# Values and scores of every fourth visit in one gap, and projected blocks copied out by ScalarE ahead of the rotary steps on VectorE

## The chip, the cores and the metric

The kernel runs on one core of one Trainium2 chip. The metric is the device time of one execution in microseconds (us); several executions are timed and their median is given. Engines are named as in the profile: PE (TensorE; PEld is its weight load), DVE (VectorE), ACT (ScalarE), POOL (GpSimd), SP (SyncE, which issues most transfers).

## The reference

A "macaron" transformer block on x of 4 x 1024 tokens with 256 features, in float32:

```
x = x + 0.5 * moe(layernorm(x))     # 32 experts, inner size 96, every expert computed for every token,
                                    # weighted by a thresholded top-8 softmax of x @ gate_weight.T
x = x + attention(layernorm(x))     # 16 query heads, 4 key/value heads, head size 16, rotary q and k,
                                    # softmax(q k^T / 4) v over 1024 keys, then Wo
x = x + 0.5 * moe(layernorm(x))
```

An expert computes `silu(x @ Wg.T) * (x @ Wu.T)`, its result goes through its down weights and is scaled by the token's weight for that expert. The rotary step replaces q by `q * cos + rotate_half(q) * sin`, and k likewise.

## The kernel before, in words

**Slots.** Both expert layers together are 384 slots (`SLOTS`), 24 for each group of 512 tokens (`PER_GROUP`); k is the group index d // 24 and s = d % 24 the slot within it. In slot d PE issues three blocks of 12 matmuls: the gate projection of step d+1 (line 1211, PSUM bank `B_G`), the up projection of step d+1 (line 1211, bank `B_U`) and the down projection of step d-1 (line 1229). ACT takes tanh of the gate result (line 668), DVE multiplies (`gated`, line 937, then `product`, line 945), POOL weighs by the expert's weight (line 601), ACT rounds to 16 bits (line 675), POOL forms the remainder (line 606), and the down projection uses both.

**Gaps and visits.** Attention runs in the gaps between these blocks: gap 0 after the gate block, gap 1 after the up block, gap 2 after the down block. One visit v is half a step of attention. PE issues two score matmuls for the row maxima of fill v + 40 (`score_max`, line 1241, 48 rows of the array) and, in other rows of the array at the same time, two score matmuls for the exponentials of v (`score_exp`, line 1253, 50 rows). DVE reduces each of the two banks of the first kind (`maximum`, line 960), ACT takes exponentials from each of the two banks of the second kind (line 691). A score matmul waits until the last contents of its bank have been taken, half by half (`max_taken`, `exp_done`). On every visit with v % 4 == 1 PE first issues two "quads" of the values (line 1274: four tiles of 32 array columns over all 128 rows, float32), and then the visit's scores. The table `VISIT` says which gap has which visit: three visits a slot while v < 0 (only maxima), then two a slot (gaps 0 and 1) and a third in gap 2 in every fifth slot. `SLOT_OF` is its inverse, and the slots for loads, output turns and output projections follow from it. The visits lie in slots 64 to 310.

**Events.** An event at the end of a slot uses bank `B_U` (`B_O` outside the attention), one ahead of the down block uses `B_G`. The event "join" projects normalised rows to one of three blocks of a group of 512 tokens (block 0: keys and values, blocks 1 and 2: queries; line 1193), in the slots s = 8, 10, 13 of k = 1 and 2 and s = 10, 12, 14 of k = 3 to 8. The next user of its bank on PE waits for `j_taken`: for `B_U` this is the up block of the next slot.

**The join on DVE.** At the end of the join's slot DVE waits for the projection, transposes the values out of PSUM for block 0 (line 918), and computes three products out of PSUM: `rb` = J * cos (line 922) and the two halves of `turned` = the swapped halves of J * sin (lines 923 and 925), the last of which sets `j_taken`. In the next slot, right behind `product`, `rope_sum` adds the two (line 932). One slot later ACT and POOL split the sum into two 16-bit parts (`rope_high`, `rope_low`), and SP stores them. There is one buffer `rb` and one `turned`.

**Order on each engine.** Each engine runs its program strictly in its own order. DVE's order in slot d is: residual add; maxima of gap 0; gated and product of step d+1; `rope_sum`; maxima of gap 1; the event of the down block; maxima of gap 2; then the work behind the last maxima, the slot's tail: output normalisation, layer norm pieces (four pieces in s = 2 to 5 and four in s = 6, 7, 9, 11), routing pieces (s = 18, 19, 20), and at the very end the event of the slot's end (the join, the logits, an output add). ACT's order is: tanh of step d+1, exponentials of gap 0, rounding of step d, `rope_high`, exponentials of gaps 1 and 2, events.

Of the kernel before, what the change touches and what calls it, by code (L numbers as in the profile page):

```python
# [7 lines left out]
ALU = mybir.AluOpType  # L8
ACT = mybir.ActivationFunctionType
# [6 lines left out]
P = 128  # L16
# [58 lines left out]
FIRST = 2 * PER_GROUP + 16  # L75


def visit_table():

    at, v, d = {}, -AHEAD, FIRST  # L80
    while v < VISITS + 2:
        for pos in range(3 if v < 0 or (d - FIRST) % 5 == 4 else 2):
            if v < VISITS + 2:
                at[d, pos] = v
                v += 1
        d += 1
    return at


VISIT = visit_table()  # L90
SLOT_OF = {v: d for (d, pos), v in VISIT.items()}


def head_of(fill):
# [105 lines left out]
def build(nc, x, wgu, wd, wg, wq, wk, wv, wo, ident_c, ktab_c, kneg_c, out):  # L200
    with ExitStack() as ctx:
# [191 lines left out]
        def _(sp):  # L393
# [50 lines left out]
            def tables(g):  # L444

                cols = slice(g % 2 * GROUP, g % 2 * GROUP + GROUP)
                if g:
                    sp.wait_ge(j_taken, JOINS * g)
                for t, v in enumerate((kcos, ksin)):
                    sp.dma_start(v, ktab_c[t, :, cols]).then_inc(tab_in, 16)  # L450

# [189 lines left out]
        def _(act):  # L641
# [52 lines left out]
            def event(d, i):  # L694

                bank = event_bank(d, i)
                name, n, j = EVENTS[d][i]
                if name in ("p_hi", "p_lo"):
                    take_rows(norm_of_join(n), n % 2, name == "p_lo", bank)
                if name in ("t_hi", "t_lo"):  # L700
                    take_rows(norm_of_group(n), n % 2, name == "t_lo", bank)
# [31 lines left out]
            for d in range(-1, SLOTS + 2):  # L733
                k, s = divmod(d, PER_GROUP)
                if d + 1 < SLOTS:
                    gate(d + 1)
                if (d, 0) in VISIT:
                    visit(VISIT[d, 0])
                if 0 <= d < SLOTS:
                    high(d)  # L740
                if d in D_HIGH_AT:
                    d_high(D_HIGH_AT.index(d) + 1)
                if d == 1 or d == 3:
                    gu_high((d + 3) // 2)
                if 1 <= k <= GROUPS:
                    if s == 6:
                        rows_high(norm_of_join(k - 1))
                    if s - 2 in join_slots(k):
                        rope_high(k - 1, join_slots(k).index(s - 2))
                if 0 <= k < PREPS - 1:  # L750
                    if s == steps_of_norm(k)[2]:
                        rows_high(norm_of_group(k + 1))
                    if s == T_LOGITS + 1:
                        exponentials(k + 1)
                if (d, 1) in VISIT:
                    visit(VISIT[d, 1])
                if len(EVENTS[d]) > 1:
                    event(d, 1)
                if (d, 2) in VISIT:
                    visit(VISIT[d, 2])  # L760
                if EVENTS[d]:
                    event(d, 0)

# [2 lines left out]
        def _(dve):  # L766
# [140 lines left out]

            HALF = 2.0 ** 3 / XW

            def join(g, piece, bank):  # L910
                dve.wait_ge(j_done, JOINS * g + piece + 1)
                J = PS[:, bank, :]
                n, m = P if piece else K_ROWS, JOINS * g + piece
                if piece == 0:
                    dve.wait_ge(tab_in, 32 * (g + 1))
                    if g:
                        dve.wait_ge(vb_out, g * 64)
                    dve.transpose(v_turned, J[K_ROWS:, :]).then_inc(v_set, 1)
                if m:
                    dve.wait_ge(qo_lo_done, m)  # L920
                link.many((
                    dve.scalar_tensor_tensor(rb[0:n, :], J[0:n, :], HALF, kcos[0:n, :], ALU.mult, ALU.mult),  # L922
                    dve.scalar_tensor_tensor(turned[0:n // 2, :], J[n // 2:n, :], -HALF, ksin[n // 2:n, :],  # L923
                                             ALU.mult, ALU.mult)))
                dve.scalar_tensor_tensor(turned[n // 2:n, :], J[0:n // 2, :], HALF, ksin[0:n // 2, :],  # L925
                                         ALU.mult, ALU.mult).then_inc(j_taken, 1)
                dve.wait_ge(v_set, g + 1)

            def rope_sum(g, piece):
                n, m = P if piece else K_ROWS, JOINS * g + piece  # L930
                dve.wait_ge(j_taken, m + 1)
                dve.tensor_tensor(rb[0:n, :], rb[0:n, :], turned[0:n, :], ALU.add).then_inc(rope_done, 1)

            def gated(d):
# [47 lines left out]
                        turn_outputs(q // QT)  # L982


            def unit_ends(v):

                f = v + AHEAD
                if f < VISITS and f % FILLS == FILLS - 1:
                    max_rows(f // FILLS)

            def turn_outputs(hv):

# [34 lines left out]
            def event(d, i):  # L1027

                bank = event_bank(d, i)
                name, n, j = EVENTS[d][i]  # L1030
                if name == "logits":
                    route(n, 0, bank)
                if name == "join":
                    join(n, j, bank)
                if name == "out_y":
                    add_outputs(n, j, bank)

# [57 lines left out]
            for d in range(-1, SLOTS + 2):  # L1095
                k, s = divmod(d, PER_GROUP)
                if d % PER_HALF == 1 and d > 1:
                    add_dense(d // PER_HALF - 1)
                if (d, 0) in VISIT:
                    visit(VISIT[d, 0])  # L1100
                if d + 1 < SLOTS:
                    gated(d + 1)
                    product(d + 1)
                if (d, 0) in VISIT:
                    unit_ends(VISIT[d, 0])
                if s - 1 in join_slots(k):
                    rope_sum(k - 1, join_slots(k).index(s - 1))
                if d == -1 or d == 0:
                    split_piece(1, d + 1)
                if d in D_LOW_AT:  # L1110
                    split_d(D_LOW_AT.index(d) + 1)
                if d in (2, 3, 5, 6):
                    split_piece(2 + d // 5, (d - 2) % 3)
                if d == 8:
                    split_small()
                if d == SPLIT_BY - 1:
                    dve.memset(vst_f, 0.0).then_inc(ones_set, 1)
                    dve.wait_ge(ones_set, 1)
                    dve.memset(vst[:, :, :, HD:HD + 1], XW / 2.0 ** 6).then_inc(ones_set, 1)
                if (d, 1) in VISIT:  # L1120
                    visit(VISIT[d, 1])
                if len(EVENTS[d]) > 1:
                    event(d, 1)
                if (d, 2) in VISIT:
                    unit_ends(VISIT[d, 1])
                    visit(VISIT[d, 2])
                if d in OUT_AT:
                    normalise(OUT_AT.index(d))
                if d - 2 in OUT_AT:
                    turn_back(OUT_AT.index(d - 2))  # L1130
                if 1 <= k <= GROUPS and 2 <= s < 6:
                    if s == 2:
                        dve.wait_ge(x_done, 2 * k)
                    norm(norm_of_join(k - 1), k - 1, s - 2, k + 1)
                if 0 <= k < PREPS - 1:
                    if s in steps_of_norm(k)[0]:
                        norm_of(k + 1, steps_of_norm(k)[0].index(s))
                    if s == T_LOGITS + 1:
# [10 lines left out]
                if (d, 2) in VISIT:  # L1149
                    unit_ends(VISIT[d, 2])  # L1150
                elif (d, 1) in VISIT:
                    unit_ends(VISIT[d, 1])


        @block.tensor
        def _(pe):
# [208 lines left out]
            for d in range(-1, SLOTS + 1):  # L1365
                if d + 1 < SLOTS:
                    gate_or_up(d + 1, 0)
                if (d, 0) in VISIT:
                    visit(VISIT[d, 0])
                if d + 1 < SLOTS:  # L1370
                    gate_or_up(d + 1, 1)
                if (d, 1) in VISIT:
                    visit(VISIT[d, 1])
# [4 lines left out]
                if (d, 2) in VISIT:  # L1378
                    visit(VISIT[d, 2])
                if EVENTS[d]:  # L1380
                    event(d, 0)

# [52 lines left out]
```

## Time and profile before

| | |
|---|---|
| median of 3 runs | 2270.76 us (2270.74 to 2271.02) |
| profiled execution | 2270.94 us, its span 2269.1 us |
| granted TensorE clock | 1.00 |
| PE busy | 2200.3 us (97%), 18794 matmuls |
| DVE busy | 1626.9 us (72%) |
| ACT busy | 1166.9 us (51%) |
| POOL busy | 1072.5 us (47%) |

Matmuls are pipelined: the profile gives a block of matmuls a busy time that reaches beyond the start of the next block, so that time lost on PE is best read from the distances of starts in the timeline.

### The profile page before, as it was taken

What the parts mean: (1) busy time and instruction counts of PE and PEld (TensorE: products, weight loads), DVE (VectorE), ACT (ScalarE), POOL (GpSimd) and SP (SyncE); (2) the same over time, 40 slices, a digit from 0 to 9 for tenths busy, and PEclk for the clock granted to TensorE, in tenths of its full rate; (3) what the DMA queues carried; (4) which work ended last, traced back from release to release, by engine and by line L of the source; (5) the groups of instructions that cost most, each with busy time, mean ns of one, the idle gap of its engine ahead of it and who ended that gap; (6) DMA issues with size and microseconds to landing.
All of it is one profiled execution on the core that took longest, in us unless ns stands there. A gap on an engine that the chain in (4) does not pass through costs nothing.

```text
span 2269.1 us, 47149 instructions
## 1 busy us (share of the span) xinstructions
PE 2200.3 (97%) x18794; PEld 1487.7 (66%) x18794; DVE 1626.9 (72%) x3203; ACT 1166.9 (51%) x1885; POOL 1072.5 (47%) x908
## 2 busy tenths in 40 slices
PE   3999999999999999999999999999999999999998
PEld 2888875556565565565566566566655665688887
DVE  7756678887887877787877877777777754454543
ACT  4433331666556556565556565566656556433332
POOL 1767654444444444444434443434344334466655
PEclk9999999999999999999999999999999999999999
DMA  5211121011111120110211111010110110101010
GB/s 222 80 41 37 39 58 31 23 42 31 35 31 43 33 51 25 34 37 24 53 41 32 31 36 32 20 42 16 26 47 6 29 32 20 30 26 40 22 40 20
DMA packets 157956, 88.50 MB, mean 39 GB/s; under 512 B 103588, under 2 KB 149924, under 8 KB 156968
## 3 DMA queue, kind: packets, MB, share of 16 engines
q1 hardware_dynamic: 157592, 85.45, 14.1%
q8 instruction: 148, 2.42, 0.4%
q14 instruction: 72, 0.59, 0.1%
q10 hardware_dynamic: 144, 0.03, 0.0%
HBM read 63.14 MB, written 11.80 MB: 33 GB/s over the span
## 4 chain that ended last, share of the span: by engine, by line
PE 89%; DVE 7%; DMA 1%; issue 1%; ACT 1%; POOL 1%; SPq 0%; POOLq 0%; DVEq 0%
PE PS L1211 43%; PE PS L1229 21%; PE PS L1241 11%; PE PS L1274 10%; DVE arena L960 2%; PE PS L1193 1%; PE PS L1303 1%; DMA X<-wd 1%; PE PS L1253 1%; DVE arena L937 1%; DVE arena L945 1%; PE PS L1179 0%; DVE turned L923 0%; DVE turned L925 0%; DVE arena L922 0%
## 5 line engine op out<-in xcount | busy, mean ns | idle before, releaser
L1211 PE MATMUL PS<-XT,WGU 128*128 128x256 f16 x9216 | 1112.0, 273 | 14.2 <-DVE turned L925 8.8
L1211 PEld LDWEIGHTS PS<-XT,WGU 128*128 128x128 f16 x9216 | 875.9, 98 | 236.9 <-issue 129.9
L606 POOL TENSOR_TENSOR arena<-arena 128x512 f16<-128x512 f32 x384 | 451.2, 1175 | 1065.9 <-ACT arena L675 1065.9
L960 DVE TENSOR_REDUCE arena<-PS 128x1 f32<-128x512 f32 x1024 | 656.5, 684 | 269.3 <-PE PS L1241 265.4
L691 ACT ACTIVATE arena<-PS,fac 128x512 f32<-128x512 f32 x1024 | 647.4, 685 | 270.7 <-PE PS L1253 270.5
L668 ACT ACTIVATE arena<-PS,fac 128x512 f32<-128x512 f32 x384 | 264.4, 689 | 771.7 <-PE PS L1211 771.7
L1229 PE MATMUL PS<-WD,arena 128*128 128x256 f16 x4608 | 568.3, 273 | 2.6 <-POOL arena L606 2.4
L601 POOL TENSOR_TENSOR arena<-arena 128x512 f32<-128x512 f32 x384 | 501.7, 1306 | 85.9 <-DMA arena<-ce_scratch 44.5
L1229 PEld LDWEIGHTS PS<-WD,arena 128*128 128x128 f16 x4608 | 430.4, 98 | 145.6 <-issue 94.6
L937 DVE SCALAR_TENSOR_TENSOR arena<-arena,PS 128x512 f32<-128x512 f32 x384 | 261.2, 680 | 247.4 <-ACT arena L668 246.6
L1241 PE MATMUL PS<-arena 48*128 48x512 f16 x1024 | 318.9, 382 | 14.9 <-DVE arena L960 12.8
L1253 PE MATMUL PS<-arena 50*128 50x512 f16 x1024 | 315.9, 382 | 0.0
L945 DVE SCALAR_TENSOR_TENSOR arena<-arena,PS 128x512 f32<-128x512 f32 x384 | 263.8, 687 | 29.7 <-PE PS L1211 12.8
L675 ACT ACTIVATE arena<-arena 128x512 f16<-128x512 f32 x384 | 242.0, 630 | 16.1 <-POOL arena L601 15.9
L1274 PE MATMUL PS<-arena 128*32 128x512 f32 x2048 | 246.2, 598 | 0.0
L1241 PEld LDWEIGHTS PS<-arena 48*128 48x128 f16 x1024 | 62.1, 94 | 216.6 <-issue 124.7
L1274 PEld LDWEIGHTS PS<-arena 128*32 128x32 f32 x2048 | 53.4, 109 | 103.6 <-issue 93.4
L1253 PEld LDWEIGHTS PS<-arena 50*128 50x128 f16 x1024 | 63.6, 93 | 15.1 <-issue 10.9
L583 POOL TENSOR_TENSOR XS<-XN,XS 128x1024 f16<-128x1024 f32 x23 | 49.0, 2131 | 0.0
L839 DVE TENSOR_SCALAR XN<-X,mv,rstd 128x256 f32<-128x256 f32 x96 | 43.8, 517 | 0.0
L843 DVE BATCH_NORM_STATS2 stats<-X 128x6 f32<-128x256 f32 x96 | 33.4, 411 | 3.1 <-DMA X<-x 3.1
L1303 PE MATMUL PS<-WO,arena 128*128 128x256 f16 x256 | 33.3, 273 | 0.2 <-DVE arena L937 0.2
(117 smaller groups left out, 729.5 us busy)
## 6 DMA issues: line engine op xcount, KB each, us to landing
arena<-ce_scratch SPq DMA_DIRECT2D x256, 128.0 KB, 3.2
arena<-wgu SPq DMA_DIRECT2D x4, 1536.0 KB, 13.4
arena<-q_scratch SPq DMA_DIRECT2D x192, 32.0 KB
arena<-ktab_c SPq DMA_DIRECT2D x16, 256.0 KB, 4.0
q_scratch<-arena SPq DMA_DIRECT2D x32, 128.0 KB, 1.8
out<-X SPq DMA_DIRECT2D x8, 512.0 KB, 3.0
X<-wd SPq DMA_DIRECT2D x2, 1536.0 KB, 24.0
X<-x SPq DMA_DIRECT2D x1, 3072.0 KB, 12.1
```

The lines of the kernel that those rows point to most:

```text
L601: pool.tensor_tensor(t, t, c, ALU.mult).then_inc(w_done, 1)
L606: pool.tensor_tensor(hs[1][:, d % HS, :], tw[d % 2], hs[0][:, d % HS, :], ALU.subtract).then_inc(lo_done, 1)
L668: act.activation(z_f, PS[:, B_G, :], ACT.Tanh, scale=F_TANH).then_inc(z_done, 1)
L691: act.activation(pex[:, v % RING * 2 + half, :], PS[:, B_EXP + half, :], ACT.Exp, scale=F_EXP).then_inc(exp_done, 1)
L937: dve.scalar_tensor_tensor(z_f, z_f, 1.0, PS[:, B_G, :], ALU.add, ALU.mult).then_inc(v_done, 1)
L945: dve.scalar_tensor_tensor(tw[d % 2], z_f, G_U_UP, PS[:, B_U, :], ALU.mult, ALU.mult).then_inc(t_done, 1)
L960: dve.tensor_reduce(mx[:, half * REP * QT + c:half * REP * QT + c + 1], PS[:, B_MAX + half, :], AX_X, ALU.max).then_inc(max_taken, 1)
L1211: ins = pe.matmul(PS[:, b, j * HALF_G:(j + 1) * HALF_G], WGU[w][:, kt, part * CHUNKS + c + j, :], XT[r][:, k % 2, kt, half * HALF_G:(half ...
L1229: ins = pe.matmul(PS[:, B_Y, i * HID:(i + 1) * HID], hs[r][:, d % HS, at:at + P], WD[w][:, d % PER_HALF * 2 + j, :], start=(first and j == ...
L1241: pe.matmul(PS[:, B_MAX + half, :], qst[64 * par:64 * par + 48, slot, i, t * P:(t + 1) * P], kst[64 * par:64 * par + 48, slot, half * 512: ...
L1253: pe.matmul(PS[:, B_EXP + n % 2, :], kst[64 * par:64 * par + 50, slot, k * P:(k + 1) * P], qst[64 * par:64 * par + 50, slot, head // 2, ha ...
L1274: ins = pe.matmul(PS[32 * head:32 * head + 32, B_O, :], vst[:, u % 2, k, :], pex[:, (2 * q + r // 2) % RING * 2 + r % 2, :], start=(k == 0 ...
```

## The change

The visit table is laid out anew. The first 40 visits stay one to a gap. From v = 0 on the visits advance by 15 gaps for 11 visits (the same 2.2 visits a slot), but a visit with v % 4 == 1 goes into the gap of the visit ahead of it. In such a gap PE issues the scores of v-1, the two quads of values, and the scores of v. The other gaps have one visit or none, in gap 0, 1 or 2 alike. In slots s = 10 to 16 of k = 4, for example, the gaps hold [none, (64, 65), none], [none, 66, 67], [(68, 69), none, none], [70, 71, none], [(72, 73), none, 74], [none, 75, (76, 77)], [none, none, 78].

The join's block is copied from PSUM to `rb` by ACT at the end of the join's slot, and this copy sets `j_taken`. DVE then works from `rb` alone, in the slot behind the join's: `rope_partners` (the two products by sin) right behind `product`, where `rope_sum` stood, and `rope_sum` at the end of the slot behind all tail work: for block 0 the transpose of the values, then `rb` * cos in place, and the add. The reload of the tables of cos and sin waits for `rope_done` in place of `j_taken`.

```
 def visit_table():
-    at, v, d = {}, -AHEAD, FIRST
-    while v < VISITS + 2:
-        for pos in range(3 if v < 0 or (d - FIRST) % 5 == 4 else 2):
-            if v < VISITS + 2:
-                at[d, pos] = v
-                v += 1
-        d += 1
+    at, gap = {}, 3 * FIRST
+    for v in range(-AHEAD, 0):
+        at[divmod(gap, 3)] = (v,)
+        gap += 1
+    for v in range(VISITS + 2):
+        where = divmod(gap + (v - (v % 4 == 1)) * 15 // 11, 3)
+        at[where] = at.get(where, ()) + (v,)
     return at
...
 # SP, tables(g)
-                    sp.wait_ge(j_taken, JOINS * g)
+                    sp.wait_ge(rope_done, JOINS * g)
...
 # ACT, event(d, i)
+                if name == "join":
+                    m = JOINS * n + j
+                    act.wait_ge(j_done, m + 1)
+                    if m:
+                        act.wait_ge(qo_lo_done, m)
+                    act.activation(rb, PS[:, bank, :], ACT.Copy).then_inc(j_taken, 1)
...
 # ACT, slot d
-                if (d, 0) in VISIT:
-                    visit(VISIT[d, 0])
+                for v in VISIT.get((d, 0), ())[:1]:
+                    visit(v)
                 if 0 <= d < SLOTS:
                     high(d)
+                for v in VISIT.get((d, 0), ())[1:]:
+                    visit(v)
...
 # DVE
-            def join(g, piece, bank):
-                dve.wait_ge(j_done, JOINS * g + piece + 1)
-                J = PS[:, bank, :]
+            def rope_partners(g, piece):
                 n, m = P if piece else K_ROWS, JOINS * g + piece
+                dve.wait_ge(j_taken, m + 1)
                 if piece == 0:
                     dve.wait_ge(tab_in, 32 * (g + 1))
+                link.many((
+                    dve.scalar_tensor_tensor(turned[0:n // 2, :], rb[n // 2:n, :], -HALF, ksin[n // 2:n, :],
+                                             ALU.mult, ALU.mult),
+                    dve.scalar_tensor_tensor(turned[n // 2:n, :], rb[0:n // 2, :], HALF, ksin[0:n // 2, :],
+                                             ALU.mult, ALU.mult)))
+
+            def rope_sum(g, piece):
+                n = P if piece else K_ROWS
+                if piece == 0:
                     if g:
                         dve.wait_ge(vb_out, g * 64)
-                    dve.transpose(v_turned, J[K_ROWS:, :]).then_inc(v_set, 1)
-                if m:
-                    dve.wait_ge(qo_lo_done, m)
-                link.many((
-                    dve.scalar_tensor_tensor(rb[0:n, :], J[0:n, :], HALF, kcos[0:n, :], ALU.mult, ALU.mult),
-                    dve.scalar_tensor_tensor(turned[0:n // 2, :], J[n // 2:n, :], -HALF, ksin[n // 2:n, :],
-                                             ALU.mult, ALU.mult)))
-                dve.scalar_tensor_tensor(turned[n // 2:n, :], J[0:n // 2, :], HALF, ksin[0:n // 2, :],
-                                         ALU.mult, ALU.mult).then_inc(j_taken, 1)
-                dve.wait_ge(v_set, g + 1)
-
-            def rope_sum(g, piece):
-                n, m = P if piece else K_ROWS, JOINS * g + piece
-                dve.wait_ge(j_taken, m + 1)
+                    dve.transpose(v_turned, rb[K_ROWS:, :]).then_inc(v_set, 1)
+                    dve.wait_ge(v_set, g + 1)
+                link(dve.scalar_tensor_tensor(rb[0:n, :], rb[0:n, :], HALF, kcos[0:n, :], ALU.mult, ALU.mult))
                 dve.tensor_tensor(rb[0:n, :], rb[0:n, :], turned[0:n, :], ALU.add).then_inc(rope_done, 1)
...
 # DVE, slot d
-                if (d, 0) in VISIT:
-                    visit(VISIT[d, 0])
+                for v in VISIT.get((d, 0), ())[:1]:
+                    visit(v)
                 if d + 1 < SLOTS:
                     gated(d + 1)
+                for v in VISIT.get((d, 0), ())[1:]:
+                    visit(v)
+                if d + 1 < SLOTS:
                     product(d + 1)
...
                 if s - 1 in join_slots(k):
-                    rope_sum(k - 1, join_slots(k).index(s - 1))
+                    rope_partners(k - 1, join_slots(k).index(s - 1))
...
                 if EVENTS[d]:
                     event(d, 0)
+                if s - 1 in join_slots(k):
+                    rope_sum(k - 1, join_slots(k).index(s - 1))
```

The loops of PE and the remaining places of ACT and DVE now run over the group of visits that a gap holds.

## Rows read from the trace of the kernel before

**Rows 1.** The page: busy times, and the chain that ended last.
```profile
PE 2200.3 (97%) x18794; PEld 1487.7 (66%) x18794; DVE 1626.9 (72%) x3203; ACT 1166.9 (51%) x1885; POOL 1072.5 (47%) x908
...
PE 89%; DVE 7%; DMA 1%; issue 1%; ACT 1%; POOL 1%; SPq 0%; POOLq 0%; DVEq 0%
```

**Rows 2.** Waits, whole span: who waited for whom, us in total, times, longest.
```profile
PE PS L1241 <- DVE arena L960: 12.8, 40, 0.9
...
PE PS L1211 <- DVE turned L925: 8.8, 13, 1.2
```

**Rows 3.** Timeline of PE: start us, duration us, what, count.
```profile
1001.50 1.48 PE L1229 MATMUL PS<-WD,arena 128*128 128x256 f16 x12
1002.82 1.47 PE L1211 MATMUL PS<-XT,WGU 128*128 128x256 f16 x12
1004.23 0.39 PE L1241 MATMUL PS<-arena 48*128 48x512 f16 x1
...
1010.02 1.49 PE L1211 MATMUL PS<-XT,WGU 128*128 128x256 f16 x12
1011.43 1.92 PE L1274 MATMUL PS<-arena 128*32 128x512 f32 x16
1013.29 0.39 PE L1241 MATMUL PS<-arena 48*128 48x512 f16 x1
...
1013.83 1.48 PE L1229 MATMUL PS<-WD,arena 128*128 128x256 f16 x12
```

**Rows 4.** Timeline of all engines behind a join of k = 4.
```profile
602.84 1.47 PE L1211 MATMUL PS<-XT,WGU 128*128 128x256 f16 x12
603.04 0.72 DVE L918 STREAM_TRANSPOSE arena<-PS 64x512 f32<-64x512 f32 x1 [1.02 <-PE PS L1193]
...
604.24 0.39 PE L1241 MATMUL PS<-arena 48*128 48x512 f16 x1
...
604.35 0.69 ACT L668 ACTIVATE arena<-PS,fac 128x512 f32<-128x512 f32 x1 [2.88 <-PE PS L1211]
...
605.93 1.29 DVE L960 TENSOR_REDUCE arena<-PS 128x1 f32<-128x512 f32 x2
606.05 1.47 PE L1211 MATMUL PS<-XT,WGU 128*128 128x256 f16 x12 [1.20 <-DVE turned L925]
...
607.14 0.68 DVE L937 SCALAR_TENSOR_TENSOR arena<-arena,PS 128x512 f32<-128x512 f32 x1
...
607.85 0.69 DVE L945 SCALAR_TENSOR_TENSOR arena<-arena,PS 128x512 f32<-128x512 f32 x1
...
610.86 1.88 DVE L839 TENSOR_SCALAR XN<-X,mv,rstd 128x256 f32<-128x256 f32 x4
```

**Rows 5.** The same timeline of PE, behind the next join.
```profile
619.73 0.39 PE L1241 MATMUL PS<-arena 48*128 48x512 f16 x1
...
620.80 1.47 PE L1211 MATMUL PS<-XT,WGU 128*128 128x256 f16 x12 [0.47 <-DVE turned L925]
622.20 0.39 PE L1241 MATMUL PS<-arena 48*128 48x512 f16 x1
...
622.69 0.39 PE L1241 MATMUL PS<-arena 48*128 48x512 f16 x1
```

**Rows 6.** Windows: slots 11 to 15 of k = 3 to 8 summed; last row later attention.
```profile
sum 227.16, PE 214.08 PEld 126.44 DVE 195.97 ACT 127.86 POOL 106.71; mean PE 35.68 PEld 21.07 DVE 32.66 ACT 21.31 POOL 17.78
...
1330.15:1968.07 637.92, 633.85 (x5323) 386.21 (x5321) 442.60 (x864) 382.89 (x628) 257.73 (x228) 1.00 0.10 27
```

**Rows 7.** The tile `turned`: duration ns min/median/max, first and last start.
```profile
L923 DVE SCALAR_TENSOR_TENSOR turned<-PS,arena x24: 681/692/694, 185.5 to 1292.4; 64x512 f32<-64x512 f32 x16, 32x512 f32<-32x512 f32 x8
...
L932 DVE TENSOR_TENSOR arena<-arena,turned x24: 641/728/1079, 188.3 to 1296.4; 128x512 f32<-128x512 f32 x16, 64x512 f32<-64x512 f32 x8
```

**Rows 8.** Timeline of DVE in a routing slot: its tail's first instruction, the next maxima.
```profile
1003.24 0.09 DVE L897 MATCH_VALUE_LOAD XN<-XN,pr 128x8 f32 x1
...
1005.12 1.25 DVE L960 TENSOR_REDUCE arena<-PS 128x1 f32<-128x512 f32 x2
```

More of the change, by code:

```diff
@@ L78, in visit_table @@
 def visit_table():
-    at, v, d = {}, -AHEAD, FIRST
-    while v < VISITS + 2:
-        for pos in range(3 if v < 0 or (d - FIRST) % 5 == 4 else 2):
-            if v < VISITS + 2:
-                at[d, pos] = v
-                v += 1
-        d += 1
+    at, gap = {}, 3 * FIRST
[5 more added lines that the diff above has]
+        at[where] = at.get(where, ()) + (v,)
     return at
 VISIT = visit_table()
-SLOT_OF = {v: d for (d, pos), v in VISIT.items()}
+SLOT_OF = {v: d for (d, pos), group in VISIT.items() for v in group}
 def head_of(fill):
@@ L754, in _ @@
                         exponentials(k + 1)
-                if (d, 1) in VISIT:
-                    visit(VISIT[d, 1])
+                for v in VISIT.get((d, 1), ()):
+                    visit(v)
                 if len(EVENTS[d]) > 1:
                     event(d, 1)
-                if (d, 2) in VISIT:
-                    visit(VISIT[d, 2])
+                for v in VISIT.get((d, 2), ()):
+                    visit(v)
                 if EVENTS[d]:
@@ L982, in visit, with unit_ends @@
                         turn_outputs(q // QT)
[L985 to L989, printed above, removed]
+            def unit_ends(visits):
+                for v in visits:
+                    f = v + AHEAD
+                    if f < VISITS and f % FILLS == FILLS - 1:
+                        max_rows(f // FILLS)
             def turn_outputs(hv):
@@ L1032, in event @@
                     route(n, 0, bank)
-                if name == "join":
-                    join(n, j, bank)
                 if name == "out_y":
@@ L1098, in _ @@
                     add_dense(d // PER_HALF - 1)
-                if (d, 0) in VISIT:
-                    visit(VISIT[d, 0])
+                for v in VISIT.get((d, 0), ())[:1]:
+                    visit(v)
                 if d + 1 < SLOTS:
                     gated(d + 1)
+                for v in VISIT.get((d, 0), ())[1:]:
+                    visit(v)
+                if d + 1 < SLOTS:
                     product(d + 1)
-                if (d, 0) in VISIT:
-                    unit_ends(VISIT[d, 0])
+                unit_ends(VISIT.get((d, 0), ()))
                 if s - 1 in join_slots(k):
-                    rope_sum(k - 1, join_slots(k).index(s - 1))
+                    rope_partners(k - 1, join_slots(k).index(s - 1))
                 if d == -1 or d == 0:
@@ L1119, in _ @@
                     dve.memset(vst[:, :, :, HD:HD + 1], XW / 2.0 ** 6).then_inc(ones_set, 1)
-                if (d, 1) in VISIT:
-                    visit(VISIT[d, 1])
+                for v in VISIT.get((d, 1), ()):
+                    visit(v)
                 if len(EVENTS[d]) > 1:
@@ L1124, in _ @@
                 if (d, 2) in VISIT:
-                    unit_ends(VISIT[d, 1])
-                    visit(VISIT[d, 2])
+                    unit_ends(VISIT.get((d, 1), ()))
+                    for v in VISIT[d, 2]:
+                        visit(v)
                 if d in OUT_AT:
@@ L1148, in _ @@
                     event(d, 0)
[L1149 to L1152, printed above, removed]
+                if s - 1 in join_slots(k):
+                    rope_sum(k - 1, join_slots(k).index(s - 1))
+                unit_ends(VISIT[d, 2] if (d, 2) in VISIT else VISIT.get((d, 1), ()))
         @block.tensor
@@ L1367, in _ @@
                     gate_or_up(d + 1, 0)
-                if (d, 0) in VISIT:
-                    visit(VISIT[d, 0])
+                for v in VISIT.get((d, 0), ()):
+                    visit(v)
                 if d + 1 < SLOTS:
                     gate_or_up(d + 1, 1)
-                if (d, 1) in VISIT:
-                    visit(VISIT[d, 1])
+                for v in VISIT.get((d, 1), ()):
+                    visit(v)
                 if len(EVENTS[d]) > 1:
@@ L1377, in _ @@
                     down(d - 1)
-                if (d, 2) in VISIT:
-                    visit(VISIT[d, 2])
+                for v in VISIT.get((d, 2), ()):
+                    visit(v)
                 if EVENTS[d]:
```

## Prediction

> **What bounds the kernel now.** First the page [rows 1]: PE is busy 97% of the span and holds 89% of the chain that ended last; DVE, at 72%, holds 7%. So time is won only where PE's stream gets shorter, and lost where PE waits, mostly for DVE. Next the waits [rows 2]: PE waited 13 times for the last product of a join (8.8 us) and 40 times for a maximum (12.8 us). Then the timeline of PE, by distances of starts [rows 3]: a block of 12 matmuls is followed by another after 1.32 us, but by scores or by quads after 1.41 us; a visit's scores take 0.54 us to the next block; two quads take 1.86 us. The 0.09 to 0.10 us by which the block ahead of other tile shapes is longer is the price of going from the whole array to 48 and 50 rows, or to 32 columns.
>
> Last the windows [rows 6], to see where DVE has room. In slots 11 to 15 of k = 3 to 8 (six stretches, 227.16 us) DVE is busy 195.97 us, 86%, and PE's idle time is 227.16 - 214.08 = 13.1 us. Later in the attention, without joins, DVE is busy 442.60 of 637.92 us (69%) and PE idles 4.1 us. The join slots are thus bound about as much by DVE as by PE: a shorter PE stream there is given back as waiting.
>
> **The merged gap.** The old table puts the visits into 554 gaps, the new one into 425, so 129 visits share a gap with the one ahead. Apart, they change shape at block to scores, scores to block, block to quads, quads to scores, scores to block: five times. Together: block to scores, scores to quads, quads to scores, scores to block: four. The trace has no scores-to-quads step. From below it costs nothing (then 0.19 us are saved each, 24 us in all), from above twice a known step, 0.19 us (nothing saved). I take the nearest rows, 0.095 us [rows 3]: 129 x 0.095 = **12.2 us saved**. The Trainium skill, TensorEngine Tiling (Array Packing), section Tiling Modes, says that a change of the tiling mode, not of the tile alone, drains the engine; by that rule the step from two row tiles to four column tiles is a change too, and the saving is the 12 us and not the 24.
>
> Does the second visit in the gap wait? Its scores start 0.53 + 1.86 = 2.39 us after the first's, while today's neighbours (scores, block, scores) are 0.54 + 1.41 = 1.95 us apart. Two maxima take 1.21 us on DVE (605.93 to 607.14, rows 4), two exponentials about the same on ACT. So nothing is lost inside a pair unless DVE is over 0.8 us late.
>
> **The join's bank.** ACT's copy out of PSUM is one 512-column activation, 0.69 us as the tanh [rows 4]; it starts when the projection has landed and ends some 0.9 us into the next gate block (1.31 us). The up block no longer waits: the 8.8 us of [rows 2] go. In k = 4 the old waits are, by starts: 606.05 - 604.24 - 0.54 = 1.27 us [rows 4]; in the next join's slot 620.80 - 619.73 - 0.54 = 0.53 us, and 0.49 - 0.23 = 0.26 us at the following visit, whose second maximum bank is late [rows 5]; behind the third join 0.53 us again. That is 2.6 us. Read in the same way, the six groups lose about **16 us** of PE's starts (the 13.1 us of idle time in [rows 6] is less because a block's modelled end reaches past the next start). ACT has the room: 16 us for 24 copies, at 51% busy [rows 1].
>
> **What is late instead.** DVE's work stays the same per join: 0.75 us transpose for block 0, three products, one add. It now lies wholly in the slot behind the join: partners 2 x 0.71 = 1.4 us between `product` and the maxima of gap 1, and at the end of the slot's tail 1.3 us (block 0: 2.1 us). In s = 11 this tail also has the layer norm's last piece, 1.8 us (four instructions, 1.88 us with the last end, rows at 610.86) [rows 4], so 3.9 us in all. I work k = 4, t = 0 at the gate block behind the first join, with steps from [rows 3, 4]:
> - Gate to 1.3, up to 2.6, scores 66 at 2.7, down, scores 67 at 4.66. DVE: tanh lands at 2.2, gated to 2.9, product to 3.6, partners to 5.0, maxima of 66 at 5.66 and 6.27. The two halves of 67 must wait for these banks: 1.06 + 0.37 = 1.4 us lost.
> - Maxima of 67 to 7.45, layer norm to 9.25, rotary sum to 11.4. PE reaches scores 68 at 8.05 and, behind the quads, 69 at 10.45; the maximum of 68 is taken at 12.1 and 12.75: 2.05 us lost.
> - Behind the second join (gaps 70, 71, then (72, 73)): 0.5 us. Behind the third (75, then (76, 77)): partners delay 75 as above, 1.4 us.
>
> Together 5.4 us against 2.6. The other groups by the same steps: k = 3 and 8 (14, then 15, (16, 17); twice a slot of 18, 19) 6.4 each; k = 5 2.9; k = 6 3.4; k = 7 2.9. Sum 27.4 us, against 16: **11.4 us lost**. Bounds: 16 us better, if the work hides wholly, and as much as 12 us worse than that sum, if each of 18 joins loses 0.7 us more. Tried on the old order at 435 us (k = 3, s = 11) such steps gave 0.9 us for a stall that the starts show as 1.2, so they don't overrate.
>
> The products also read two SBUF tensors now, where they read PSUM before. The PSUM forms take 681 to 694 ns in every one of 24; the add, the only one of the group with two SBUF inputs, takes 641 to 1079, mean about 0.1 us more [rows 7]. Three products x 18 joins x 0.1 = 5.4 us on DVE; about a fifth reaches PE: **1 us**, ends 0 and 5. The Trainium skill, VectorE: DVE Perf Modes, section "Two Vector instructions with no wait between them", says that the second of two SBUF inputs is read through an interface shared with GpSimd; by it the spread of the add is POOL's doing, and the moved products would show the same.
>
> **Other tails.** If maxima in gap 2 are followed by one in gap 0 and another in gap 1, or by one in gap 1 and one in gap 2, DVE has only 1.4 to 2.0 us for the tail before PE waits. Counting starts in the tables, 8 of 20 slots are so now, 4 of 20 before (the other 16 left 2.8 us or more). Routing tails are about 1.9 us [rows 8], three per group, ten groups: 30 x (0.4 - 0.2) x 0.8 us (0.4 late, plus 0.37 at the second bank) = 5 us, less 2 us for the slots with three visits that are gone: **3 us lost**, ends -4 and +10 (the 12.8 us of waits for maxima in [rows 2] could go to zero in part, or double).
>
> The moved waits: the reload of the tables waits for the last sum, a slot or more ahead of SP's place for it; the values' store on SP is behind `rope_high`'s slot as before; ACT's copy waits for POOL's remainder of the join before, which ends in the copy's own slot before the projection does (in k = 4 at 15.5 us against 17). Behind that copy ACT has the tanh, and behind `rope_high`, which waits for DVE's sum, only exponentials that PE itself is late for. Nothing added, 0 to 3 us.
>
> **Sum.** On the profiled execution's 2270.94 us (2269.1 us span and 1.8 us around it; 0.2 us above the median of the runs): -12.2 + 11.4 + 1 + 3 = +3.2, so 2274.1, and 0.2 less against the median: **2274 us**.
>
> **Rivals.**
> - *The waits for DVE go.* The bank is free early, DVE's rotary work fills its idle time, and later slots have room (69% busy). For: PE's idle time at joins in the old trace is nearly all named after the join. Against: 86% busy there, and the partners stand ahead of the maxima. It gives -12.2 and about half of the 8.8 us: 2254 to 2262, say 2258.
> - *The rotary lateness carries on.* Place: DVE's end of s = 11, where 1.8 us of layer norm and 2.1 us of rotary sum stand ahead of the maxima of s = 12. If the six stretches together keep PE waiting over 33 us (16 + 12.2 + 4.5), the kernel is slower. With 0.7 us more for each of 18 joins: 2274 + 12 = 2286; with half of it 2280.
> - *Scores to quads is free.* Then 12 us more are saved: 2262.
> - *The saving is not made*, because quads start only when the exponentials of v-2 are there, and these are now a gap nearer. ACT has them 1.2 us after their scores, the quads come at least 2.5 us after: unlikely, 2286.
>
> **How the numbers follow.** Within 0.2% (4.5 us; about what can be told from no change) lies the sum, 2266.2 to 2275.3: 0.40. Slower: the carried lateness 0.31, the saving not made 0.03, together 0.34. Faster: the waits that go 0.21, the free step 0.05, together 0.26. The range for 8 in 10 reaches into both: 2258 to 2285; the likeliest case alone is 2266 to 2276.
>
> **What would show it.** Scores behind a block, then quads, scores and a block with 0.53 us between the first scores and the quads (0.44 if the step is free). No wait of line 1211 for a join's copy. PE's waits for maxima grow from 12.8 us to some 30. In s = 12 of k = 4 the second visit of the pair starts about 2 us late. The prediction is wrong if PE's waits for maxima don't grow (then about 2255), or if the DVE stalls are seen in slots without joins.

## The result, and the profile after

The changed kernel takes 2356.26 us (median of 5 runs, 2353.49 to 2357.89) against 2270.76 us: 1.0376 times as long, 95% interval 1.0361 to 1.0392, or 85.5 us more. The forecast was 2274 us, with a range up to 2285.

The page of the changed kernel, as [rows 1] of before:

```profile
span 2355.8 us, 47174 instructions
...
PE 2221.3 (94%) x18794; PEld 1507.6 (64%) x18794; DVE 1664.7 (71%) x3203; ACT 1190.2 (51%) x1909; POOL 1075.5 (46%) x908
...
PE 80%; DVE 14%; issue 2%; DMA 1%; POOL 1%; ACT 1%; SPq 0%; POOLq 0%; DVEq 0%; ACTq 0%
```

PE idles 134.5 us (span less busy time), 68.8 before, so 65.7 us of the span's growth of 86.7 are idle time and 21.0 are busy time. DVE's share of the last chain has doubled. PE's waits, as [rows 2] (us in total, times, longest); line 1252 is `score_max`, 970 the maximum, 1222 the gate and up blocks, 947 `gated`:

```profile
PE PS L1252 <- DVE arena L970: 67.6, 82, 3.6
PE PS L1222 <- DVE arena L947: 14.8, 14, 2.8
```

The waits for a join's bank are gone, as forecast. Those for maxima are 67.6 us, not some 30, and PE now waits for `gated` too. Where the time is lost, first in windows over the same slots as [rows 6] (11 to 15 of k = 3 to 8); columns: length, busy us and count of PE, PEld, DVE, ACT, POOL, granted clock, DMA share, GB/s:

```profile
452.95:498.73 45.78, 36.67 (x266) 21.44 (x264) 33.49 (x48) 21.69 (x35) 19.43 (x15) 0.91 0.12 25
630.02:680.21 50.19, 42.81 (x306) 23.47 (x305) 37.01 (x54) 24.50 (x40) 18.80 (x15) 0.90 0.16 31
...
981.95:1022.38 40.43, 35.73 (x286) 21.10 (x284) 33.18 (x50) 23.34 (x38) 17.28 (x15) 1.00 0.14 27
...
sum 280.38, PE 232.60 PEld 132.32 DVE 210.59 ACT 136.66 POOL 108.55; mean PE 38.77 PEld 22.05 DVE 35.10 ACT 22.78 POOL 18.09
```

280.38 against 227.16 us: 53.2 us of the loss are in these thirty slots, where PE's idle time went from 13.1 to 47.8 us and DVE was busy 14.6 us more. The other 18.5 us are PE's own busy time, in stretches whose granted clock fell. The next windows are k = 1 and 2 up to slot 72, then k = 9 to 12, first of the changed kernel, then of the one before:

```profile
146.18:378.37 232.19, 220.18 (x1911) 178.21 (x1908) 163.03 (x315) 76.20 (x120) 138.15 (x112) 0.99 0.18 45
1437.34:2064.52 627.18, 619.22 (x5243) 386.62 (x5240) 430.85 (x837) 376.37 (x612) 255.42 (x226) 1.00 0.10 26
```
```profile
146.29:366.02 219.73, 217.86 (x1910) 177.96 (x1908) 155.34 (x315) 72.28 (x114) 137.80 (x112) 1.00 0.19 48
1350.18:1977.89 627.71, 623.64 (x5243) 381.87 (x5240) 431.25 (x837) 373.14 (x612) 254.93 (x226) 1.00 0.10 26
```

k = 1 and 2, which have joins and almost no visits, lose 12.5 us, of which PE waits 10.1 us for `gated` (none before); k = 9 to 12, with visits and no joins, gain 0.5. The span's growth is 86.7 us, so 86.7 - 53.2 - 12.5 + 0.5 = 21.5 us are in the other slots of k = 3 to 8.

The place worked in the prediction, k = 4 behind the first join (PE, DVE and POOL; gate block at 630.02):

```profile
632.97 0.69 DVE L955 SCALAR_TENSOR_TENSOR arena<-arena,PS 128x512 f32<-128x512 f32 x1
...
633.69 0.82 DVE L929 SCALAR_TENSOR_TENSOR turned<-arena 32x512 f32<-32x512 f32 x1
633.93 1.71 POOL L604 TENSOR_TENSOR arena<-arena 128x512 f32<-128x512 f32 x1
634.54 1.64 DVE L931 SCALAR_TENSOR_TENSOR turned<-arena 32x512 f32<-32x512 f32 x1
636.22 2.58 DVE L970 TENSOR_REDUCE arena<-PS 128x1 f32<-128x512 f32 x4
...
636.96 0.39 PE L1252 MATMUL PS<-arena 48*128 48x512 f16 x1 [2.20 <-DVE arena L970]
```

`product` ends at 633.66, 3.6 us after the gate block's start, as worked out. But the two partner products end at 636.18 and not at 635.1: the second takes 1.64 us, beside POOL's weighing (line 604), which starts 0.27 us after `product` ends, 0.61 us ahead of the second product, and is itself stretched to 1.71 us. The scores of 67 start 6.94 us after the gate block, 5.72 had been expected.

In this trace the granted clock is 0.987 in the mean, 1.00 before. Windows of k = 8, s = 12:

```profile
1343.00:1347.00 4.00, 0.77 (x6) 0.22 (x3) 3.90 (x8) 1.47 (x3) 1.64 (x2) 1.00 0.00 0
1347.00:1352.00 5.00, 3.70 (x18) 0.68 (x18) 4.86 (x7) 1.53 (x3) 4.02 (x3) 0.66 0.02 5
```

PE did nothing for 3.1 us, waiting for a maximum, and in the stretch behind it the clock fell to its lower level, 1.2 GHz, for part of the time: the quads there took 3.38 us, 1.92 elsewhere. Over the span the clock cost at most 2355.8 x 0.013 = 31 us (an estimate: half speed costs half of the time spent at it, if PE was always busy there). It comes on top of the waits.

### The profile page after: what moved, and what is told of

Same layout as the page of the kernel before. It is cut to its first block, busy times and chain, and to the rows that moved or that the text cites. A ratio compares the mean times of both kernels' runs of the same rounds, so it can differ in the third digit from the quotient of the medians.

```text
span 2355.8 us, 47174 instructions
## 1 busy us (share of the span) xinstructions
PE 2221.3 (94%) x18794; PEld 1507.6 (64%) x18794; DVE 1664.7 (71%) x3203; ACT 1190.2 (51%) x1909; POOL 1075.5 (46%) x908
## 4 chain that ended last, share of the span: by engine, by line
PE 80%; DVE 14%; issue 2%; DMA 1%; POOL 1%; ACT 1%; SPq 0%; POOLq 0%; DVEq 0%; ACTq 0%
PE PS L1222 38%; PE PS L1240 19%; PE PS L1252 10%; PE PS L1285 9%; DVE arena L970 4%; DVE turned L931 2%; DVE arena L947 2%; PE PS L1204 1%; PE PS L1314 1%; DMA X<-wd 1%; PE PS L1264 1%; DVE arena L955 1%; DVE turned L929 1%; DVE XN L850 1%; ACT arena L671 1%
## 5 line engine op out<-in xcount | busy, mean ns | idle before, releaser
L1222 PE MATMUL PS<-XT,WGU 128*128 128x256 f16 x9216 | 1100.1, 274 | 21.3 <-DVE arena L947 14.8
L1240 PEld LDWEIGHTS PS<-WD,arena 128*128 128x128 f16 x4608 | 440.3, 98 | 116.8 <-issue 61.0
L1252 PE MATMUL PS<-arena 48*128 48x512 f16 x1024 | 327.1, 386 | 69.7 <-DVE arena L970 67.6
L1264 PE MATMUL PS<-arena 50*128 50x512 f16 x1024 | 324.1, 386 | 0.0
L955 DVE SCALAR_TENSOR_TENSOR arena<-arena,PS 128x512 f32<-128x512 f32 x384 | 263.4, 686 | 35.0 <-issue 11.7
L1285 PE MATMUL PS<-arena 128*32 128x512 f32 x2048 | 253.8, 614 | 0.0
L591 POOL TENSOR_TENSOR arena<-arena 128x512 f16<-128x512 f32 (+1 forms) x24 | 27.7, 1156 | 31.6 <-ACT arena L685 31.6
L931 DVE SCALAR_TENSOR_TENSOR turned<-arena 64x512 f32<-64x512 f32 (+1 forms) x24 | 39.4, 1644 | 0.7
```

Source lines behind the costliest of these rows:

```text
L955: dve.scalar_tensor_tensor(tw[d % 2], z_f, G_U_UP, PS[:, B_U, :], ALU.mult, ALU.mult).then_inc(t_done, 1)
L1222: ins = pe.matmul(PS[:, b, j * HALF_G:(j + 1) * HALF_G], WGU[w][:, kt, part * CHUNKS + c + j, :], XT[r][:, k % 2, kt, half * HALF_G:(half ...
L1240: ins = pe.matmul(PS[:, B_Y, i * HID:(i + 1) * HID], hs[r][:, d % HS, at:at + P], WD[w][:, d % PER_HALF * 2 + j, :], start=(first and j == ...
L1252: pe.matmul(PS[:, B_MAX + half, :], qst[64 * par:64 * par + 48, slot, i, t * P:(t + 1) * P], kst[64 * par:64 * par + 48, slot, half * 512: ...
L1264: pe.matmul(PS[:, B_EXP + n % 2, :], kst[64 * par:64 * par + 50, slot, k * P:(k + 1) * P], qst[64 * par:64 * par + 50, slot, head // 2, ha ...
L1285: ins = pe.matmul(PS[32 * head:32 * head + 32, B_O, :], vst[:, u % 2, k, :], pex[:, (2 * q + r // 2) % RING * 2 + r % 2, :], start=(k == 0 ...
```

## Experiments

Times are medians; each ratio is to the kernel before, with its 95% interval. Differences below are to the kernel before as it was timed beside each run (2270.5 to 2270.8 us).

| kernel | us | ratio (interval) |
|---|---|---|
| new table alone | 2303.16 | 1.0145 (1.0130 to 1.0161) |
| rotary change alone | 2332.73 | 1.0272 (1.0257 to 1.0287) |
| - partners at the slot's start | 2281.96 | 1.0055 (1.0039 to 1.0072) |
| - all of it at the slot's start | 2304.30 | 1.0147 (1.0132 to 1.0162) |
| - partners first, sum behind `product` | 2300.95 | 1.0133 (1.0118 to 1.0148) |
| - as changed, POOL's weighing waits | 2308.81 | 1.0168 (1.0154 to 1.0181) |
| the whole change, POOL's weighing waits | 2330.88 | 1.0266 (1.0252 to 1.0280) |
| old table, pairs in the earlier gap | 2297.16 | 1.0114 (1.0097 to 1.0131) |
| old table, pairs in the later gap | 2278.41 | 1.0034 (1.0023 to 1.0046) |
| new spacing, no pairs | 2299.69 | 1.0129 (1.0114 to 1.0144) |
| old table, 73 pairs where DVE is free | 2261.26 | 0.9958 (0.9945 to 0.9972) |
| the same, values' rows copied by ACT | 2268.15 | 0.9987 (0.9978 to 0.9996) |

### The two halves of the change

**The new visit table, the old join.**
```
 # visit_table(), loops over groups of visits: as changed
-# ACT's copy, rope_partners, late rope_sum
+# DVE's join out of PSUM and rope_sum, as before
```


> The new visit table alone; the join stays on DVE as before. Groups k = 9 to 12 of the changed kernel, which have visits but no joins, took as long as before (a step of -0.6 us over four groups, where the removed switches should give -3.8). Theory 1 (the rotary parts cost the 85 us): within 5 us of before, 2266 to 2276. Rival (the merged gaps leave DVE too little time for its tails and so make the loss): 2300 or more, with a granted clock under 1.

+32.7 us, mean clock 0.997: the rival's numbers. The table costs much by itself. Its trace, as [rows 2]:

```profile
PE PS L1249 <- DVE arena L967: 29.3, 59, 4.4
PE PS L1219 <- DVE turned L932: 18.0, 16, 1.7
```

Both old waits have more than doubled, from 12.8 and 8.8 us. The second, because where gap 0 behind a join is empty the up block wants its bank 1.31 us after the gate block's start and not 1.95 (k = 4, s = 11):

```profile
606.77 1.47 PE L1219 MATMUL PS<-XT,WGU 128*128 128x256 f16 x12
609.98 1.47 PE L1219 MATMUL PS<-XT,WGU 128*128 128x256 f16 x12 [1.74 <-DVE turned L932]
```

1.9 us lost by starts, 1.27 before [rows 4].

**The rotary change, the old table.**
```
 # ACT's copy, rope_partners, late rope_sum: as changed
-        at[where] = at.get(where, ()) + (v,)
+                at[d, pos] = (v,)        # the old positions, one visit each
```


> The rotary change alone (copy by ACT, partners and sum on DVE as in the changed kernel), with the old visit table. Theory 1: 2330 to 2360, with the second partner product at 1.64 us in all 24 and waits of PE for maxima behind joins; groups k = 1 and 2, which have no visits, lose 12 us as in the changed kernel. Rival (table): near 2282, the 12 us of groups 1 and 2 and nothing more.

+62.2 us, as theory 1 had it, so both halves cost, the rotary one more; PE's waits for maxima are 51.0 us in 78. The halves add to 94.9 us, the change has 85.5: the new table lengthens the waits for the join's bank by 9.2 us, and with ACT's copy these waits don't exist.

### Why the rotary parts cost

**Partners at the start of the slot.**
```
 # DVE, slot d
+                if s - 1 in join_slots(k):
+                    rope_partners(...)
                 ... maxima of gap 0, gated, product ...
-                if s - 1 in join_slots(k):
-                    rope_partners(...)
```


> The rotary change alone, but with the two partner products at the start of the slot, ahead of the maxima of gap 0 and of the tanh step, where DVE otherwise waits and POOL does not weigh; the sum stays at the slot's end. Theory 1a (the partners are slow because POOL's weighing starts with them): the second product falls from 1.64 to 0.7 us, POOL's weighing beside it from 1.7 to 1.27, and the time falls by 20 us or more against the rotary change alone. Rival 1b (the operands make it slow, whatever runs beside it): it stays 1.64 us. If the sum at the end is what costs, the time stays over 2300.

50.8 us less than with the partners behind `product`. The tile `turned` (ns min/median/max), first of the rotary change alone, then of this kernel:

```profile
L931 DVE SCALAR_TENSOR_TENSOR turned<-arena x24: 681/1644/1654, 188.1 to 1354.0; 64x512 f32<-64x512 f32 x16, 32x512 f32<-32x512 f32 x8
```
```profile
L931 DVE SCALAR_TENSOR_TENSOR turned<-arena x24: 681/685/771, 185.1 to 1303.9; 64x512 f32<-64x512 f32 x16, 32x512 f32<-32x512 f32 x8
```

(Before, out of PSUM: 679/683/685.) PE's waits for maxima fall from 51.0 to 22.7 us. Place and length both changed here, so:

**POOL's weighing waits for the partners; nothing is moved.**
```
 # POOL, slot d
+                if s - 1 in join_slots(k):
+                    pool.wait_ge(partners_done, ...)
                 if d + 1 < SLOTS:
                     weigh(d + 1)
...
 # DVE, rope_partners: each product counts up partners_done, then
+                dve.wait_ge(partners_done, 2 * m + 2)
```


> The rotary change alone, old visit table, everything in its place; only POOL's weighing of the step waits until DVE's two partner products are done, so that the two don't run at once. The rotary change alone took 2332.7 us, with the second product at 1.64 us. If POOL beside it makes it slow: both products 0.69 us, 24 x 1.3 us = 31 us less work on DVE, of which 15 to 30 reach the end: 2303 to 2318. If the place in DVE's order is the whole cost, no change: 2330 or more, since POOL now starts later.

> The changed kernel with the same one wait: POOL's weighing behind the partner products. It took 2356.3 us. By the same reason 2325 to 2340, and the granted clock rises from 0.987 to 0.99 or more, since the long waits of PE get shorter. If the product's length does not matter: 2350 or more.

23.9 us less in the rotary change, 25.4 us less in the whole change (mean clock 0.992 for 0.987), though nothing was moved and waits were only added, for POOL and for DVE behind its own two products. The second product in the rotary change with this wait:

```profile
L933 DVE SCALAR_TENSOR_TENSOR turned<-arena x24: 681/685/687, 188.2 to 1336.1; 64x512 f32<-64x512 f32 x16, 32x512 f32<-32x512 f32 x8
```

So POOL beside it is what makes the product slow: 24 x 0.96 = 23 us of DVE, against 24 to 25 us of the kernel's time. The first product stays stretched (median 1027 ns): it runs beside POOL's remainder step. Of the 50.8 us that the partners' earlier place gave back, some 24 are thus their length, and the other 27 their place between `product` and the maxima of gap 1.

**All rotary work at the slot's start.**
```
 # DVE, slot d: first
+                    rope_partners(...)
+                    rope_sum(...)
```


> The rotary change alone, with partners, cos product and add all at the start of the slot. DVE's order is then about the old one, but the bank is free early. Theory 1 (place and neighbours cost, not the copy by ACT): 2255 to 2272, at or under before, PE's 8.8 us of waits for the join gone. Rival (the copy through ACT itself costs, by its wait for POOL's remainder of the join before): over 2280.

The rival's number, not its reason: in all 24 the copy waited for the projection (36.7 us), never for POOL. DVE starts 0.63 us later than the old join, since ACT must copy first, and works 2.8 us or more (block 0: 3.5 us) ahead of the maxima of gap 0 and of `gated`: PE waits 31.6 us for maxima and 11.7 for `gated`.

**Partners first, the sum right behind `product`.**
```
-                # at the slot's end: rope_sum(...)
+                # behind product(d + 1): rope_sum(...)
```


> Rotary change alone, old visit table, the two partner products at the start of the slot and the sum (transpose, cos product, add) right behind product, in place of the slot's end. With the sum at the end this took 2282, with 16 us of PE's waits in s = 12, behind the layer norm piece and the sum of s = 11. If those waits come from the sum's place at the end, 2262 to 2276. But the sum now starts with POOL's weighing: if two SBUF inputs beside POOL are what is slow, the cos product or the add takes 1.6 us there, and the time is 2280 or more.

2300.95 us, the second branch: the add, now beside POOL, has a median of 1638 ns; 692 with the sum at the end. Place and length changed together again: DVE is busy 16.7 us more (1653.8 against 1637.1), so the 19 us lost don't show which place would be better without POOL.

### Why the table costs

**Pairs without the new spacing, in the earlier or the later of the two gaps; the new spacing without pairs.**
```
+                if v > 0 and v % 4 == 1:
+                    at[last] += (v,)                     # earlier
+                    at[d, pos] = at.pop(last) + (v,)     # or: later
                 else:
                     at[d, pos] = (v,)
```
```
-        where = divmod(gap + (v - (v % 4 == 1)) * 15 // 11, 3)
+        where = divmod(gap + v * 15 // 11, 3)            # spacing alone
```


> The old positions of the visits and the old join; only each visit with v % 4 == 1 is put into the gap of the visit ahead of it, its own gap stays empty. 128 switches fewer, 12 us of PE's stream. If the spreading of the visits over gap 2 made the table's loss of 33 us (theory), this kernel comes to 2258 to 2268. If a pair in one gap is what makes DVE late (rival), it stays over 2290.

> As the kernel that merges into the earlier gap, but merged into the later one: the first of the pair waits for its partner's gap. Theory (the spreading costs, not the pairs): 2258 to 2270. Rival (pairs cost): over 2290. Between the two merged kernels it shows whether it matters that DVE gets its next maximum later.

> The new spacing of 15 gaps for 11 visits, over gaps 0, 1 and 2 alike, but no visit merged, with the old join. No switch is saved. Theory (spreading costs): 2290 to 2310, the joins and routing slots waiting as with the new table. Rival (pairs cost): 2265 to 2275.

The theory that only the spacing costs falls, and so does the rival that only the pairs do: pairs in the earlier gap cost 26.4 us, in the later 7.7, although each saves the 12 us of switches (2278 us lies in neither expected range); the spacing alone costs 29.0 (its waits for the join's bank are 17.9 us). The two don't add: 29.0 + 26.4 is more than the table's 32.7. A pair in the later-gap kernel, k = 4, s = 7, PE and then DVE:

```profile
569.13 0.39 PE L1253 MATMUL PS<-arena 48*128 48x512 f16 x1
...
569.66 1.92 PE L1286 MATMUL PS<-arena 128*32 128x512 f32 x16
574.57 0.61 PE L1253 MATMUL PS<-arena 48*128 48x512 f16 x1 [2.99 <-DVE arena L971]
```
```profile
569.55 2.08 DVE L981 SCALAR_TENSOR_TENSOR arena<-arena 128x32 f16<-128x32 f32 x1
...
572.43 1.36 DVE L852 BATCH_NORM_STATS2 stats<-X 128x6 f32<-128x256 f32 x4
573.83 1.29 DVE L971 TENSOR_REDUCE arena<-PS 128x1 f32<-128x512 f32 x2
```

From the first scores to the quads are 0.53 us, as forecast, and not 0.44: the rival of a free step falls. The pair's second scores could start 1.86 us behind the quads, at 571.52, and start at 574.57: DVE was still in the tail of the slot before. In the kernel before, with the same 2.07 us instruction in that tail, PE waited 0.85 us here. Apart, the two visits' scores are 0.54 + 1.41 + 1.86 = 3.81 us apart at a visit with quads, in a pair 2.39. The 1.4 us of block between them was DVE's time to catch up. This kernel executes the same DVE instructions as before, yet they are busy 1643.3 us, 16.4 more; how much of its loss comes from instructions that thus got longer was not tested.

**Pairs only where DVE is free.**
```
+                if v > 0 and v % 4 == 1 and d % PER_GROUP not in (5, 6, 7, 10, 11, 12, 13, 19, 20, 21):
+                    at[d, pos] = at.pop(last) + (v,)
```


> The old join and the old positions; a visit with v % 4 == 1 shares its gap with the visit ahead (both in the later gap) only in slots s = 0 to 4, 8, 9, 14 to 18, 22 and 23, where DVE's tail ahead of the pair is short: 73 pairs of 129. Theory (a pair costs only where a tail or a join comes ahead of it, elsewhere it saves a switch of 0.095 us): 73 x 0.095 = 6.9 us less, 2263 to 2266. Rival (pairs shift the lateness to other slots): 2269 or more.

2261.26 us, the best of all, 9.5 us under the kernel before. Page and PE's waits:

```profile
PE 2190.1 (97%) x18794; PEld 1491.6 (66%) x18794; DVE 1627.4 (72%) x3203; ACT 1166.1 (52%) x1885; POOL 1073.0 (47%) x908
```
```profile
PE PS L1253 <- DVE arena L971: 12.5, 40, 0.9
...
PE PS L1223 <- DVE turned L936: 9.3, 13, 1.2
```

PE's busy time falls by 10.2 us and the waits stay about those of before (12.8 and 8.8). 73 switches of 0.095 us are 6.9 us; the time is 2 us under the expected range, and these rows don't show where the other 2.6 us come from.

**The same, and the values' rows taken out of PSUM by ACT.**
```
+                    act.activation(rb[K_ROWS:, :], PS[K_ROWS:, bank, :], ACT.Copy).then_inc(v_copied, 1)
-                    dve.transpose(v_turned, J[K_ROWS:, :])     # DVE, in the join
+                    dve.transpose(v_turned, rb[K_ROWS:, :])    # DVE, in rope_sum
```


> The kernel with 73 merged pairs, and of the rotary change only this: for block 0 ACT copies the values' 64 rows of the join out of PSUM, and DVE transposes them from SBUF in the next slot, ahead of the rotary add; the three products stay on DVE, out of PSUM, at the slot's end. The bank is held 0.75 us shorter behind each of the 8 first joins, of which 6 lie in the attention (old waits there 1.26 us, behind the other joins 0.53). Theory: 3 to 5 us less, 2256 to 2259, and the 1.26 us waits fall to 0.5. Rival (what the transpose adds to the next slot comes back as waits for maxima in s = 12, as in the rotary change): 2260 to 2266.

The rival, and worse: 6.9 us more than without it. The bank waits fall from 9.3 to 6.6 us, those for maxima rise from 12.5 to 18.0: what left the join came back one slot later, with 2.7 us won and 5.5 lost. These rows are of one of the two fastest of 11 executions (2265.12 us, clock 1.00), 4.0 us more than without the copy; the median execution has a clock of 0.998 and is 3 us longer still.

## Why the prediction was wrong, step by step

- *The merged gap saves 12.2 us*: the price of a switch was right, by the 0.53 us between scores and quads and by the kernel with 73 pairs; in the changed kernel's k = 9 to 12 PE's busy time is 4.4 us less. What failed is the paragraph behind it. It set the pair's 2.39 us against 1.95 us of "today's neighbours" and so found more room than before; but the two visits of a pair had the quads between them, and were 3.81 us apart. And that nothing is lost unless DVE is over 0.8 us late was no comfort without a count of how often it is.
- *The join's bank*: right, the 8.8 us are gone.
- *Other tails, 3 us*. This failed step misses by the most: the table alone shows 32.7 + 12.2 saved = 45 us of waits and of lower clock (0.997). I took the room before a maximum for that of scores, block, scores, and left out the same 1.86 us of quads. In the changed kernel 21.5 us of loss are in the other slots of k = 3 to 8, where clock and joins' after-effects have a share too.
- *What is late instead, 11.4 us*: the rotary change alone costs 62.2 us; less the 24 of the next step, that is 38 in place of 11.4. k = 4 was worked to 2.8 us more waiting. Its stretch is 50.19 - 37.35 = 12.8 us longer, of which PE's idle time is 5.2; the rest is busy time, an extra visit with quads (306 matmuls, 285 before) and a clock of 0.90. By the windows' means the clock cost 3 to 5 us in five of the six stretches.
- *Two SBUF inputs: 0.1 us each, 1 us in all*. The failed step that the runs isolate best: the second product took 0.96 us more, each time, and POOL's wait alone gives back 24 to 25 us. I took the price from the mean of the add in [rows 7], whose spread has an order in it that I didn't look for. In the trace of the kernel before (first the add at 608.45 us, then a product of 128 x 32):

```profile
608.45 0.68 DVE L932 TENSOR_TENSOR arena<-arena,turned 64x512 f32<-64x512 f32 x1
608.61 1.65 POOL L601 TENSOR_TENSOR arena<-arena 128x512 f32<-128x512 f32 x1 [0.67 <-DVE arena L945]
```
```profile
570.66 2.14 POOL L583 TENSOR_TENSOR XS<-XN,XS 128x1024 f16<-128x1024 f32 x1
570.77 2.07 DVE L970 SCALAR_TENSOR_TENSOR arena<-arena 128x32 f16<-128x32 f32 x1
```

POOL's weighing ran beside 23 of the 24 adds, but always started after the add, and then POOL was the one that took longer (1.65 us for 1.27). Where DVE started second, as in the lower pair, it finished only with POOL: 2.07 us for a product that takes 0.19 alone. The partners were put where the second one starts 0.6 us after POOL, every time; it ends 0.5 us after POOL does. The Trainium skill (VectorE: DVE Perf Modes, section "Two Vector instructions with no wait between them") names the read interface shared with GpSimd, and the trace now agrees with it, 1.64 us against 0.68; that section gives no price.
- *k = 1 and 2 left out*: they lost 12.5 us. Without visits PE reaches the next gate block soon, and waits for `gated`, which DVE does behind the rotary sum of the slot before. I had only looked for maxima.
- *The clock* stood in no term: up to 31 us of PE's pace.
- *Of the rivals*, the carried lateness had the right place and sign (PE kept waiting over 33 us in the six stretches: 47.8 of idle time) and a third of the chance, but its price was a sixth of the truth.

Together: the sum had DVE's lateness at 11.4 + 1 + 3 = 15.4 us, and the runs show 85.5 + 12.2 = 98 us of lateness and of the lower clock that went with it. How this divides between the two is not settled exactly: idle time grew by 65.7 us, and the clock accounts for at most 31, but no run held the clock up with the waits in place.

## What to carry to other kernels

Where a second engine is 86% busy beside a bound engine, time between two of its due results is a resource: removing 1.4 us of the bound engine's work between them can cost more than it saves, and saves in full only where that engine has nothing else to do. Before moving work off PSUM and onto SBUF, look at what the instruction in front releases: one that reads two SBUF tensors should not start shortly behind a POOL instruction. Started ahead of it, it kept its length here, and POOL paid. Price a step in a nearly full stage by the rows of its worst neighbourhood, and check every consumer of the engine's order, not only the one that waits today.

## What the runs showed of the hardware

A DVE product of 64 x 512 or 32 x 512 with two SBUF inputs takes 0.68 us alone. Started 0.6 us behind a POOL product of 128 x 512 it takes 1.64 us, in all 24 of the changed kernel; a 128 x 32 one took 2.07 us behind a POOL instruction of 2.14 us and 0.19 alone. The one that starts second is the one that gets longer: in the kernel before, 11 adds that started 0.16 us ahead of POOL's weighing, with nothing else of POOL beside them, stayed at 0.68 to 0.69 us, and the weighing took 1.65 instead of 1.27. With one input in PSUM nothing of this shows: `product` stayed at 0.69 us wherever POOL was already running. Two SBUF inputs are not the whole condition, though: the 128 x 32 TENSOR_SCALAR ahead of that product, with one, took 1.18 us beside POOL (569.56 us of the kernel before) and 0.18 alone.

Stretches at 1.2 GHz followed waits of PE of 1.2 to 3.6 us, but not each of them: the clock was 0.66 over 415 to 420 us, behind a wait of 1.2 us, and stayed at 1.00 over 205 to 215 us, behind one of 2.8 us. The trace of the kernel before has none until its last 2 us; the mean over the 50 us of k = 4 was 0.90.
